# A graph network of two layers on one core: each weight piece is asked for only once the piece two ahead of it has landed

## The reference

```python
h = jnp.maximum(_layernorm(x, axis=-1), 0.0)
q = h @ wq.T + bq ; k = h @ wk.T + bk ; v = h @ wv.T + bv
q2 = (q @ wiq.T + biq) ; k2 = (k @ wik.T + bik) ; v2 = (v @ wiv.T + biv)   # 16 heads of 64
scores = jnp.einsum('hnd,hmd->hnm', q2, k2) * scale + mask[None]
out = jnp.einsum('hnm,hmd->hnd', jax.nn.softmax(scores, axis=-1), v2)
x = x + out @ wo.T + bo
h = jnp.maximum(_layernorm(x, axis=-1), 0.0)
u = h @ root + bias
for r in range(8):
    u = u + mean_r @ weight[r]      # mean_r: mean of h over the edges of type r into a node
z = jnp.concatenate([u, h], axis=1) @ w_gate + b_gate
x = x + jnp.tanh(u) * z + h * (1.0 - z)
```

## Time and profile before

| | us |
|---|---|
| median of 3 runs | 227.75 (226.43 to 230.03) |
| the profiled execution | 226.06 |
| its span, from the first to the last instruction | 224.3 |
| TensorE busy in it | 214.3 (96%) |
| VectorE busy | 85.1 (38%) |
| HBM read | 75.97 MB, 340 GB/s over the span |

### The profile page before, as it was taken

How to read it: one execution, slowest core, us unless ns; L and a number is a source line. 1 busy time by engine, 2 the same in 40 slices (tenths; PEclk the granted TensorE clock), 3 DMA queues, 4 the chain that set the end, 5 groups by cost and what they waited for, 6 DMA issues and landing times.

```text
span 224.3 us, 10195 instructions
## 1 busy us (share of the span) xinstructions
PE 214.3 (96%) x4789; PEld 208.5 (93%) x4789; DVE 85.1 (38%) x150; ACT 21.4 (10%) x41; POOL 25.5 (11%) x57
## 2 busy tenths in 40 slices
PE   2999989999999998999999999999999999989993
PEld 2899989999999998799999999999999999989993
DVE  2469847231699721458978500000000000000624
ACT  2432000000110120311224000000000000000101
POOL 3365006400000000010000950000000000000000
PEclk9999999999999999999999999999999999999999
DMA  6999999999999999999999999999999999994002
GB/s 217 393 382 425 424 418 394 396 321 370 359 380 378 375 348 381 396 384 412 387 348 367 384 394 359 361 340 386 402 352 380 337 367 368 361 419 188 3 3 70
DMA packets 14697, 77.02 MB, mean 343 GB/s; under 512 B 4880, under 2 KB 5152, under 8 KB 5440
## 3 DMA queue, kind: packets, MB, share of 16 engines
q1 hardware_dynamic: 14112, 75.96, 88.3%
q10 hardware_dynamic: 544, 0.42, 0.6%
HBM read 75.97 MB, written 0.39 MB: 340 GB/s over the span
## 4 chain that ended last, share of the span: by engine, by line
PE 95%; DMA 1%; issue 1%; DVE 1%; ACT 0%
PE acc L796 82%; PE acc L1040 4%; DMA x_sb<-in_x 1%; PE turn L983 1%; PE side L844 1%; PE side L983 1%; PE side L1040 1%; PE turn L872 1%; DVE stats L513 1%; PE acc L814 1%; PE turn L884 0%; PE side L855 0%; PE turn L855 0%; PE acc L884 0%; PE side L837 0%
## 5 line engine op out<-in xcount | busy, mean ns | idle before, releaser
L796 PE MATMUL acc<-mean,raw 128*64 128x96 f32 x2048 | 85.1, 246 | 0.7 <-issue 0.7
L796 PEld LDWEIGHTS acc<-mean,raw 128*64 128x64 f32 x2048 | 84.8, 137 | 0.9 <-issue 0.9
L796 PE MATMUL acc<-hT,raw 128*64 128x96 f32 x1024 | 44.7, 247 | 1.4 <-issue 1.3
L796 PEld LDWEIGHTS acc<-hT,raw 128*64 128x64 f32 x1024 | 43.0, 137 | 2.7 <-issue 2.4
L759 DVE TENSOR_TENSOR uT<-acc,uT 128x384 f32<-128x384 f32 x2 | 1.1, 558 | 82.3 <-PE acc L796 82.3
L796 PE MATMUL acc<-qT,raw 128*64 128x96 f32 x512 | 22.0, 247 | 0.0
L796 PEld LDWEIGHTS acc<-qT,raw 128*64 128x64 f32 x512 | 21.4, 137 | 0.4 <-issue 0.3
L796 PE MATMUL acc<-kT,raw 128*64 128x96 f32 x512 | 21.7, 246 | 0.0
L796 PEld LDWEIGHTS acc<-kT,raw 128*64 128x64 f32 x512 | 21.3, 137 | 0.3 <-issue 0.3
L796 PE MATMUL acc<-uT,raw 128*64 128x96 f32 x256 | 11.9, 258 | 0.0
L796 PEld LDWEIGHTS acc<-uT,raw 128*64 128x64 f32 x256 | 11.5, 146 | 0.3 <-ACT uT L415 0.2
(11 more groups left out here) (178 smaller groups left out, 148.0 us busy)
## 6 DMA issues: line engine op xcount, KB each, us to landing
raw<-in_weights SPq DMA_DIRECT2D x284, 256.0 KB, 4.8
raw<-in_weights SPq DMA_DIRECT2D x1, 1024.0 KB, 6.1
x_sb<-in_x SPq DMA_DIRECT2D x1, 192.0 KB, 3.3
x_sb<-in_x ACTq DMA_DIRECT2D x1, 192.0 KB, 3.8
out<-out_rows SPq DMA_DIRECT2D x1, 192.0 KB, 2.1
out<-out_rows ACTq DMA_DIRECT2D x1, 144.0 KB, 2.5
out<-out_rows SPq DMA_DIRECT2D x1, 48.0 KB, 2.2
bias_rows<-in_biases ACTq DMA_DIRECT2D x1, 36.0 KB
```

What stands on the lines that cost most here:

```text
L796: mm = pe.matmul(a[g * HD:(g + 1) * HD, b, c * N:(c + 1) * N], raw[:, s, at:at + HD], moving(k0 + k), start=opens and k0 == 0 and c == 0 a ...
```

## The change

In `fetch(n)`, from piece 3 on, SyncE waits for one thing more before it issues the four DMAs of piece n: that piece n-2 has landed in full. The wait for the slot stays. Nothing else is changed.

```diff
                 if n >= SLOTS:
                     sp.wait_ge(piece_used, n - SLOTS + 1)
+                if n >= 3:
+
+                    sp.wait_ge(raw_landed[(n - 2) % SLOTS], landed(n - 2))
                 for part in transfers(n):
```

## The result

| | before | changed |
|---|---|---|
| median of 6 runs | 228.05 us | 260.39 us |
| profiled execution, span | 224.3 us | 256.5 us |
| TensorE busy | 214.3 us (96%) | 221.3 us (86%) |

The changed kernel is **slower: 1.137 times the time of before** (95% interval 1.130 to 1.144; some executions of either kernel are slower for reasons outside it, and the ratios here leave them out, on both sides). The forecast was 228.0 us, with a range from 225.2 to 234.6: no change that could be told from noise. It was wrong by 32 us.

The account below looks back on a forecast made before the run. TensorE was taken to set the end; at 2.9 us a piece under the gate the stream's lead would hide it, with 0.3 us added for one late piece: 227.75 + 0.3 = 228.0 us, range 225.2 to 234.6.

Parts of the forecast that it names:

- What bounds the kernel before: TensorE, busy 96% of the span, sets the end; the weight stream runs ahead of it at 2.80 us a piece.
- The lead of 10.9 us at piece 71: Piece 71 lands at 206.2 us and TensorE asks for it at about 217.1; the gate would use 7 us of this.
- the gate binds at nearly every piece: SyncE's added wait for piece n-2 ends last nearly everywhere, holding issues back 4.1, 1.0 and 2.5 us at three places.
- The form of the cycle: Piece n lands 5.8 us after piece n-2: wake, issue spread, long issues and last landing; two pieces land in it.
- The wake: SyncE starting again once piece n-2 has landed: 0.05 us of the cycle.
- the spread: On SyncE, from a piece's first DMA issue to its fourth, three steps of 0.64 us: 1.9 us of the cycle.
- long issues: SyncE's occasional longer DMA issues: 0.25 us a piece in the cycle.
- The last term: Time from a piece's last DMA issue to its landing: 3.6 us taken, with bounds of 2.1 and 5.0 us.
- the gate becomes the pace: Rival at SyncE's wait before each piece: 3.05 us a piece, 6.8 us more, 234.6 us; chance 0.24, including paces to 3.6.
- lagging engine: Argument for the slower rival: a piece's slowest DMA takes 0.6 to 1.2 us over their median, and all engines wait.
- TensorE gains: Rival at TensorE's "issue" idles for raw: a shorter queue gives back up to 5.9 us; chance of over 2%: 0.06.
- The fit of the Trainium skill: For the weight DMAs: 4.4 us for 1.05 MB, 2.2 us a piece with two in flight, 226.1 us in the profile's terms.

Follow-up runs that it names:

- gate2_late: The changed kernel with its wait on piece n-2 only from piece 36 on: 240.11 us, 1.059 times the time of before.
- gate1: The changed kernel with the wait one piece back instead of two, so each piece travels alone: 449.71 us in a single run.
- slide8: Kernel before, with a semaphore for each of a piece's four DMAs and each DMA waiting for the one eight ahead: 228.61 us, ratio 1.007.
- slide4: Kernel before, with a semaphore for each of a piece's four DMAs and each DMA waiting for the one four ahead: 301.61 us in one run.
- one_dma_gate1: The changed kernel with one DMA of 1 MiB a piece instead of four, and the wait one piece back: 371.63 us in a single run.
- gate3: The changed kernel with the wait three pieces back instead of two: 225.78 us, 0.9985 times the time of before.
- slide6: Kernel before, with a semaphore for each of a piece's four DMAs and each DMA waiting for the one six ahead: 248.12 us, ratio 1.095.

## Why the prediction was wrong, step by step

**What bounds the kernel before: right.** The lead of 10.9 us at piece 71 and the pace of 2.80 carry the accounts above: 249.0 - 217.1 = 31.9 us late, 32.2 us measured. gate2_late spends the lead and pays the rest, as worked out.

**That the gate binds at nearly every piece: right.** 53 of the 69 waits show in SyncE's waits, and the chain goes through them. By the times of issue and landing in the trace, 66 of the 69 pieces are issued within 0.1 us of the landing of piece n-2.

**The form of the cycle: right.** The wake is 0.07 us (0.05 put down), the spread 1.79 (1.9) with about 0.2 of long issues (0.25).

**The last term, "I take 3.6, the shortest of 285": wrong, and this is the error.** 2 x 3.41 - 0.07 - 1.79 - 0.2 = 4.76 us. There were two mistakes in that choice. The first: the shortest of all 285 was the second DMA of piece 16, and for the first three of a piece the view's time is no landing of their own (see gate1), while the cycle is closed by the landing of all four. In the same trace the last DMA of a piece takes 5.5 us in the mean and 4.2 at the least. Of the five pieces in the earlier trace rows with a time to landing, none has its slowest DMA under 5.0 us. The second: the difference to 2.1 us was read as queue that the gate takes away, "some 2.6 us of the median is queue". gate1 shows 4.2 us for the last DMA with no other piece ahead. The gate made the last term shorter by 0.8 us (from 5.5 to 4.75), while it held the issue back by 1.0 to 4.1 us at the three places that the prediction looked at. The upper bound that stood in the text, the 5.0 us of piece 17 whose issue came nearest to the gate, would have given 3.6 us a piece and some 273.5 us: 5% over what was measured, and on the right side.

**The rival "the gate becomes the pace" was the truth**, with a chance of 0.24 and a price of 6.8 us. The chance was too low because the two sides were weighed by one chosen value, though by the text's own sum 0.1 us in it was worth 3.6 us at the end. The price was too low because the 6.1 us of piece 0 are those of one DMA; a piece in four DMAs with another ahead takes 6.8. The rival's paces up to 3.6, named at its end, took in the measured 3.41, but the range left them out. The "lagging engine" that spoke for it, a slowest DMA 0.6 to 1.2 us over the median of its piece, is mostly the counting of the shared semaphore: in slide8, with one for each DMA, the slowest is 0.2 us over the median in the mean, against 0.8 in the kernel before (0.6 in slide4, where the queue is short). No run tests by itself whether a laggard "catches up while the others idle".

**The rival "TensorE gains": no.** Its "issue" idles at raw are 7.1 us in 10 places under the gate (5.9 in 12 before).

**The fit of the Trainium skill** ("DMA: Bandwidth & Descriptors", the anatomy of one DMA: 2.0 us fixed plus the bytes at 436 GB/s, for the GpSimd path) gives an estimate of 4.4 us for a piece. The piece alone in one DMA takes 4.8 in the median (one_dma_gate1), so for one transfer by itself this case nearly agrees, which I had denied from a quarter piece under load. Carried over to two in flight it gives 2.2 us a piece or the engines' pace; measured were 3.09 with one DMA a piece and 3.41 with four. The 6.15 us that the Trainium skill (same page, the section on bandwidth) has for 1 MB, issued from GpSimd, lies above our 4.8.

**What stays open.** Why a 256 KB load takes some 4 us even with three or fewer others on their way (slide4, gate1) wasn't taken apart further. That packets take longer with a short queue (below) fits, but isn't shown to be the whole of it.

## What to carry to other kernels

Before a stream is throttled by "wait until k pieces ago has landed", take the time from the first issue of a piece to its last landing where the queue is shortest, and divide by k: if that isn't clearly below the pace needed, the gate is the new bound. Here piece 17 of the earlier trace rows takes 48.4 + 5.0 - 46.5 = 6.9 us, 3.45 a piece for k = 2, and 3.41 was measured. The landing that counts is that of the last DMA of a piece, which is also the only one that a shared semaphore tells. It shrinks little when the queue does (5.5 us before, 4.75 with the gate, 4.2 alone). If a limit is needed, look one piece further back (gate3, no loss) or let each DMA wait for its own counterpart (slide8, 0.7%) instead of stopping until a whole piece is in.

## What the hardware showed that I had not expected

The same 9216 packets of 8 KB took longer when fewer were queued. The page's share of the load queue times span times 16 engines is the time that packets took:

```profile
q1 hardware_dynamic: 14112, 75.96, 85.8%
```

This row is of the changed kernel, 0.858 x 256.5 x 16 = 3521 us. The page of before has 88.3% for that row, 3169 us; gate3 3205 (88.9% of 225.3), slide6 3450 (88.0% of 245.0), slide4 3751 (78.2% of 299.8), and gate1:

```profile
q1 hardware_dynamic: 14112, 75.96, 52.5%
```

0.525 x 448.0 x 16 = 3763 us, 19% more than before for the same bytes. By this account half of the lost pace is not idle engines: (3521 - 3169) / 16 / 71 = 0.31 us a piece of the 0.61 is slower packets. The kernel before fits: its first stretch, with times to landing of 6.7 to 7.4 us at piece 3, moved 406 GB/s, the later ones, with 4.2 to 6.0 at the four pieces shown, 369 and 371; but other things differ between these stretches too. So the queue before wasn't mere waiting: with a shorter one the same packets took longer.

The bytes on their way aren't all of it. slide4 and one_dma_gate1 both allow 1 MiB, and the first needs 3751 us, the second 3444 (58.2% of 369.9), with one DMA over 128 partitions in place of four over every fourth partition. What makes a packet slow wasn't found.
